# A recommender tower on one core: 24 interaction rows kept, dense features in the free rows of the pair chunks

## What is computed

```python
combined = jnp.concatenate([sparse_x, dense_x[:, None, :]], axis=1)      # 512 x 27 x 128
interact = jnp.einsum('bfd,bgd->bfg', combined, combined)
z = interact[:, _TRIU_I, _TRIU_J]                                        # 512 x 351
h = jnp.concatenate([z, r_dense_x], axis=1)                              # 512 x 479
h = jnp.maximum(h @ W_top1 + b_top1, 0.0)                                # 479 x 512
h = jnp.maximum(h @ W_top2 + b_top2, 0.0)                                # 512 x 256
y = h @ W_top3                                                           # 256 x 1
```

## Time and profile before

| | before |
|---|---|
| median of 3 runs | 120.97 us (120.47 to 121.06) |
| the profiled execution | 120.48 us |
| its span, first to last instruction | 118.7 us |
| TensorE busy | 110.9 us, 93% (weight loads 88.0, 74%) |
| VectorE busy | 93.1 us, 78% |
| ScalarE busy | 50.6 us, 43% |
| GpSimd busy | 71.6 us, 60%, none of it after 96.72 |
| granted TensorE clock | 1.0 throughout |
| moved | 13.20 MB, 111 GB/s on average |

### The profile page before, as it was taken

How to read it: one execution, slowest core, us unless ns; L and a number is a source line. 1 busy time by engine, 2 the same in 40 slices (tenths; PEclk the granted TensorE clock), 3 DMA queues, 4 the chain that set the end, 5 groups by cost and what they waited for, 6 DMA issues and landing times.

```text
span 118.7 us, 2740 instructions
## 1 busy us (share of the span) xinstructions
PE 110.9 (93%) x794; PEld 88.0 (74%) x794; DVE 93.1 (78%) x379; ACT 50.6 (43%) x147; POOL 71.6 (60%) x80
## 2 busy tenths in 40 slices
PE   4999999999999999999989999799999996999990
PEld 4844454546454799759979898699998895998980
DVE  1699999999999998984999999940689992589312
ACT  5970640506050618930355871105686104586110
POOL 3477777777777776776777777776777750000000
PEclk9999999999999999999999999999999999999999
DMA  3999757454535125897321221221221220000000
GB/s 83 303 319 383 205 168 242 76 215 88 184 111 181 51 68 96 321 355 226 72 51 46 67 45 50 52 63 45 61 59 46 61 50 0 6 0 0 0 0 1
DMA packets 6543, 13.20 MB, mean 111 GB/s; under 512 B 2033, under 2 KB 3569, under 8 KB 6401
## 3 DMA queue, kind: packets, MB, share of 16 engines
q0 software_dynamic: 2336, 4.79, 15.1%
q1 hardware_dynamic: 3328, 5.50, 13.9%
q10 hardware_dynamic: 864, 2.75, 7.5%
HBM read 13.03 MB, written 0.00 MB: 110 GB/s over the span
## 4 chain that ended last, share of the span: by engine, by line
POOL 58%; issue 19%; PE 14%; DMA 5%; POOLq 1%; DVE 1%; ACT 0%; DVEq 0%
POOL rows L329 58%; PE gram_ps L625 6%; PE h_ps L660 3%; DMA idx<-in_ids_dram 3%; DMA rows<-in_tbl_dram,idx 2%; PE turn_ps L645 2%; PE h_ps L645 1%; POOLq L102 1%; PE gram_ps L645 1%; PE turn_ps L631 0%; DVE h L485 0%; DVE h_prod L487 0%; PE turn_ps L598 0%; ACT XT L374 0%; PE gram_ps L631 0%
## 5 line engine op out<-in xcount | busy, mean ns | idle before, releaser
L329 POOL DMA_INDIRECT rows<-in_tbl_dram,idx x73 | 70.5, 966 | 24.0 <-issue 22.0
L430 DVE COPY PAIRS<-gram_ps 27x60 f32<-27x60 f32 (+1 forms) x96 | 24.3, 253 | 11.6 <-PE gram_ps L625 10.2
L625 PE MATMUL gram_ps<-XT 128*123 128x80 f32 x256 | 28.5, 269 | 1.2 <-ACT XT L374 0.9
L625 PEld LDWEIGHTS gram_ps<-XT 128*123 128x123 f32 x256 | 27.9, 188 | 2.0 <-ACT XT L374 1.4
L374 ACT COPY PAIRS<-gram_ps 27x60 f32<-27x60 f32 (+1 forms) x96 | 23.3, 243 | 10.3 <-PE gram_ps L625 9.2
L374 ACT COPY XT<-turn_ps 128x512 f32<-128x512 f32 (+3 forms) x20 | 12.2, 619 | 34.3 <-PE turn_ps L598 18.2
L455 DVE CUSTOM_DVE_ANT_0 few_prod<-rows 128x128 f32<-128x128 f32 x84 | 20.6, 289 | 0.8
L513 DVE TENSOR_SCALAR onehot<-hot_ids,first_row 125x512 bf16<-125x512 int16 (+1 forms) x64 | 19.4, 374 | 2.4 <-DMA hot_ids<-in_hot_ids_dram 2.1
L645 PE MATMUL h_ps<-PAIRS,W1P 128*128 128x128 f32 x130 | 16.8, 276 | 0.2
L645 PEld LDWEIGHTS h_ps<-PAIRS,W1P 128*128 128x128 f32 x130 | 15.5, 192 | 0.5 <-ACT PAIRS L374 0.3
L588 PE MATMUL turn_ps<-onehot,hot_tab 125*128 125x512 bf16 (+3 forms) x56 | 11.7, 351 | 0.0
(11 more groups left out here) (49 smaller groups left out, 87.0 us busy)
## 6 DMA issues: line engine op xcount, KB each, us to landing
hot_tab<-in_hot_dram ACTq DMA_DIRECT2D x5, 512.0 KB, 3.6
rows<-in_tbl_dram SPq DMA_DIRECT2D x128, 0.5 KB
W1P<-in_w_pairs_dram SPq DMA_DIRECT2D x1, 1280.0 KB, 5.9
rows<-in_tbl_dram,idx POOLq DMA_INDIRECT x73, 2.9
hot_tab<-in_hot_dram SPq DMA_DIRECT2D x2, 512.0 KB, 7.4
hot_ids<-in_hot_ids_dram SPq DMA_DIRECT2D x1, 640.0 KB, 7.5
hot_tab<-in_hot_dram SPq DMA_DIRECT2D x2, 256.0 KB, 3.4
W<-in_W_top_dram SPq DMA_DIRECT2D x1, 512.0 KB
```

The source lines that it names most:

```text
L329: pool.indirect_dma_start(rows[:, t, s, :], None, tables[f], bass.IndirectOffsetOnAxis(ap=idx[:, t, f:f + 1], axis=0)) \
L430: return nc.vector.tensor_copy(dst, src)
L625: last = nc.tensor.matmul(gram_ps[0:GRAM_ROWS, 2 * (i % 2) + q // fours, o:o + QUAD * NCOL], four.rearrange("d s f -> d (s f)")[:, 0:GRAM_ ...
```

## The change

It makes these edits:

- **24 rows.** The slots of each sample are filled in another order: dense, the fields of gather groups 1 to 6, the hot fields, and last the three fields of group 0. `move_pairs` copies 24 partitions, `gram` has 3 x 32 + 24 = 120 stationary columns. Pairs among the last three slots are in no copied row, so `FEW` grows from 21 to 24 and each part from seven pairs to eight. The pairs now come from gather groups 0, 1 and 2, not 0 and 1.
- **Free rows.** A quadrant now has eight free rows. The 24 few pairs all fit in those of chunk 0: one turn and one addition are left of two. Chunks 1 to 4 have 4 x 8 x 4 = 128 free rows, which take the dense input. Four loads on SP's queue, eight partitions and 2048 floats each, write it from `x_t`. W1's dense rows are in `W1P`; `W1D` and its product are gone. ScalarE clears chunk 0 alone.
- **First loads.** ScalarE's load of the first ids moves to SP's queue behind the index; ids come as [0], [1], [2:8] instead of [0], [1:3], [3:8]; table 2 comes ahead of the dense input. The copy of the dense input into `XT` moves behind ScalarE's fifth bank.
- **Warm-up.** Nine matmuls on a tile of zeros cleared by VectorE, in place of eight on the identity.
- **Turns of tile 0** move up: [1, 2], [3, 4], [5, 6], [].

```diff
-FEW = [(a, g) for g in range(FIRST) for a in range(g)]
+KEPT = 24
+APART = NVEC - KEPT
+FEW = [(a, g) for g in range(KEPT, NVEC) for a in range(KEPT, g)] + [(a, g) for g in range(FIRST) for a in range(g)]
...
-GRAM_ROWS = SLOTS * (QUAD - 1) + NVEC
+GRAM_ROWS = SLOTS * (QUAD - 1) + KEPT
...
-WARM_UP = 8
+WARM_UP = 9
 RING = 3
+DENSE_AFTER = 4
...
-SLOT_FIELD = [NTAB] + COLD + HOT
+ROW_FIELD = [NTAB] + COLD
+SLOT_FIELD = [NTAB] + COLD[APART:] + HOT + COLD[:APART]
+ROW_SLOT = [SLOT_FIELD.index(f) for f in ROW_FIELD]
...
-TURNS_AFTER = [[[1], [2, 3], [4, 5], [6]], [[1, 2], [3, 4], [5], []], [[1, 2], [5], [3], [4]]]
+TURNS_AFTER = [[[1, 2], [3, 4], [5, 6], []], [[1, 2], [3, 4], [5], []], [[1, 2], [5], [3], [4]]]
...
             sp.dma_start(idx[:], ids).then_inc(idx_in, 16)
+            sp.dma_start(hot_ids[:, 0, :], hot_ids_in[:, 0, :]).then_inc(ids_first_in, 16)
...
-            sp.dma_start(hot_ids[:, 1:3, :], hot_ids_in[:, 1:3, :]).then_inc(ids_next_in, 16)
+            sp.dma_start(hot_ids[:, 1, :], hot_ids_in[:, 1, :]).then_inc(ids_next_in, 16)
             load_hot(sp, 1)
+            sp.dma_start(hot_ids[:, 2:n_look, :], hot_ids_in[:, 2:n_look, :]).then_inc(ids_rest_in, 16)
+            load_hot(sp, 2)
...
             sp.dma_start(W1P[:], w1_pairs).then_inc(w1_in, 16)
-            sp.dma_start(W1D[:], w1_dense).then_inc(w1_in, 16)
+            for s in range(4):
+                sp.dma_start(PAIRS[SLOTS * s + KEPT:SLOTS * (s + 1), 1:PART_COLS, :],
+                             x_t.rearrange("(s i k) b -> s i k b", s=4, i=SPARE)[s]).then_inc(dense_pairs_in, 16)
...
-            act.dma_start(hot_ids[:, 0, :], hot_ids_in[:, 0, :]).then_inc(ids_first_in, 16)
             act.wait_ge(few_cleared, 1)
-            zero_pairs(0, PART_COLS // 2)
-            zero_pairs(PART_COLS // 2, PART_COLS)
...
+            nc.scalar.activation(PAIRS[:, 0, :].rearrange("p (t s) -> p t s", t=TILES),
+                                 few[:, 0:1, 0:P].broadcast_to([P, TILES, P]), ACT.Identity).then_inc(pairs_zero, 1)
...
-                nc.vector.tensor_tensor(PAIRS[0:SLOTS, 1, here], PAIRS[0:SLOTS, 1, here],
-                                        few_bank[t][0:SLOTS, P:2 * P], ALU.add).then_inc(turn_read["dve"], 1)
...
+            pe.wait_ge(warm_ready, 1)
+            for _ in range(WARM_UP):
+                nc.tensor.matmul(h2_ps[:, 0:P], warm[:], warm[:], start=True, stop=True)
             pe.wait_ge(ident_ready, 1)
...
-            def layer1_dense(t, n):
-                nc.tensor.matmul(h1_out(t, n), W1D[:, n * P:(n + 1) * P], denseT[:, t * P:(t + 1) * P],
-                                 start=True, stop=False)
...
-                order = list(range(FEW_CHUNKS, PART_COLS)) + list(range(FEW_CHUNKS))
+                order = [*range(1, PART_COLS), 0]
...
-                    pe.wait_ge(w1_in, 32)
+                    pe.wait_ge(w1_in, 16)
+                    pe.wait_ge(dense_pairs_in, 16 * 4)
```

More of the change, by code:

```diff
@@ L120, in build @@
         W1P = sb("W1P", [P, PART_COLS, H1], F32)
-        W1D = sb("W1D", [P, H1], F32)
         W2 = sb("W2", [P, HC1, H2], F32)
@@ L340, in empty_bank @@
                 _, n, a, b = item
-                slot = TURNED + n if n < n_hot else TURNED - 1
+                slot = SLOT_FIELD.index(LOOKUPS[n])
                 copy(XT[:, a * P:b * P, slot], ps[:, 0:(b - a) * P]).then_inc(turn_read[reader[i]], 1)
@@ L437, in few_pairs @@
                     if t == 0:
-                        dve.wait_ge(pairs_zero, 2)
+                        dve.wait_ge(pairs_zero, 1)
                     dve.wait_ge(dense_in, 16)
+                go = FEW[part * FEW_GO:(part + 1) * FEW_GO]
                 for g in range(NG):
-                    if GROUPS[g][0] < FIRST:
+                    if any(ROW_SLOT[r] in pair for r in GROUPS[g] for pair in go):
                         dve.wait_ge(gathered[g], 16 * gather_count(g) * (t + 1))
@@ L453, in few_pairs @@
                         dve.wait_ge(few_step, step - 1)
-                    col = few_place(i)[1] * P + few_place(i)[0]
+                    col = few_place(i)
                     nc.vector.tensor_tensor_reduce(
-                        out=few_prod[:, step % 2, :], in0=rows[:, t, a, :], in1=rows[:, t, g, :], scale=1.0,
+                        out=few_prod[:, step % 2, :], in0=rows[:, t, ROW_SLOT.index(a), :], in1=rows[:, t, ROW_SLOT.index(g), :], scale=1.0,
                         scalar=0.0, op0=ALU.mult, op1=ALU.add,
@@ L466, in add_few @@
                 dve.wait_ge(turned, fill_no[("few", t)] + 1)
[L467 to L469 removed]
+                nc.vector.tensor_tensor(PAIRS[:, 0, here], PAIRS[:, 0, here], few_bank[t][:, 0:P],
+                                        ALU.add).then_inc(turn_read["dve"], 1)
             def relu_dve(t, n):
@@ L551, in _ @@
         def _(pe):
+            pe.wait_ge(warm_ready, 1)
+            for _ in range(WARM_UP):
+                nc.tensor.matmul(h2_ps[:, 0:P], warm[:], warm[:], start=True, stop=True)
             pe.wait_ge(ident_ready, 1)
-            for _ in range(WARM_UP):
-                nc.tensor.matmul(h2_ps[:, 0:P], ident[:], ident[:], start=True, stop=True)
             def bank_free(i):
@@ L645, in layer1_pairs @@
                     last = nc.tensor.matmul(h1_out(t, n), W1P[:, k, n * P:(n + 1) * P], PAIRS[:, k, t * P:(t + 1) * P],
-                                            start=False, stop=(k == order[-1]))
+                                            start=(k == order[0]), stop=(k == order[-1]))
                 if t == TILES - 1 or n == HC1 - 1:
@@ L696, in _, with weight_rows @@
                         fill(late_hot)
-            pe.wait_ge(pairs_act, BATCHES * (t + 1) - 1)
-            pe.wait_ge(pairs_dve, BATCHES * (t + 1) - 1)
-            for n in range(HC1 - 1):
-                layer1_dense(t, n)
             for n in range(HC1):
-                if n == HC1 - 1:
-                    layer1_dense(t, n)
-                layer1_pairs(t, n)
+                layer1(t, n)
             layer2(t)
 def few_place(i):
-    chunk, i = divmod(i, FEW_PER_CHUNK)
     quadrant, row = divmod(i, SPARE)
-    return SLOTS * quadrant + NVEC + row, chunk
-def pair_rows():
+    return SLOTS * quadrant + KEPT + row
+def weight_rows():
     rows = []
@@ L724, in pair_rows @@
             a, g = sorted((slot[i], slot[j]))
-            if g < FIRST:
-                rows.append((*few_place(FEW.index((a, g))), n))
+            if (a, g) in FEW:
+                rows.append((few_place(FEW.index((a, g))), 0, n))
             else:
@@ L730, in pair_rows @@
             n += 1
-    return rows, n
+    for d in range(D):
+        s, i, k = d // (SPARE * (PART_COLS - 1)), d // (PART_COLS - 1) % SPARE, d % (PART_COLS - 1)
+        rows.append((SLOTS * s + KEPT + i, 1 + k, n + d))
+    return rows
 def kernel(**inputs):
@@ L760 @@
     w1 = _np.asarray(inputs["W_top1"])
-    where, n_pairs = pair_rows()
-    p, k, r = (_np.array(c) for c in zip(*where))
+    p, k, r = (_np.array(c) for c in zip(*weight_rows()))
     w1_pairs = _np.zeros((P, PART_COLS, H1), w1.dtype)
@@ L765 @@
     w1p = give("w1_pairs", w1_pairs)
-    w1d = give("w1_dense", w1[n_pairs:])
     b1 = give("b_top1", _np.asarray(inputs["b_top1"]).reshape(HC1, P).T)
@@ L771 @@
     out = nc.dram_tensor("out_0_dram", (BATCH, 1), _mybir.dt.float32, kind="ExternalOutput").ap()
-    build(nc, x, x_t, ids, row_ids, hot_ids, hot_tables, tables, w1p, w1d, b1, w2, b2, w3, out)
+    build(nc, x, x_t, ids, row_ids, hot_ids, hot_tables, tables, w1p, b1, w2, b2, w3, out)
     r = _run(nc, [arrays], core_ids=[0])
```

54 lines of the change are left out of this document (23 added, 31 removed).

## The result

The changed kernel took 126.73 us (median of 4 runs, 126.17 to 126.78), the kernel before 121.02 us (120.47 to 121.75) beside it. The ratio is 1.050, its 95% interval 1.046 to 1.054: slower by 5.7 us, where 120.9 was forecast.

What follows compares the result with a forecast made beforehand. Gathers bound the last interactions (99.42), with VectorE and TensorE close. L of 53.6 plus 46.10 starts them 0.28 late, the tail gains 0.32: -0.04, so 120.9 us against the median; range 120.4 to 121.7.

Steps and rivals of the forecast that it cites:

- Dense rows by four loads into the pair chunks: Tile 0, before layer one: W1P lands at 52.43, the dense loads at 53.5, so layer one starts at 53.6.
- L: Start of layer one in tile 0, its first pair matmul: forecast 53.6, from 53.2 to 53.8.
- the term of 1.1: Time in us by which the four dense loads land behind W1P, taken between 0.75 and 1.5.
- The bound of 1.5: Upper bound in us for the dense loads landing behind W1P, at half of W1D's rate: landing 53.95.
- Rival 2: VectorE waits in tile 0 for turn 1 behind the dense loads and passes it on: 122.0 us, chance 0.15.
- The sum along VectorE: Spans added from layer one's start in tile 0 to the last interactions: together 46.10 us.
- ready for layer one: TensorE in tile 0, after VectorE's longer first tile: ready at 53.27, where before it was 52.50.
- The tail: From the last interactions to the end: gain 0.32 us, 19.0 instead of 19.28.
- Tile 1's wait for VectorE: Sign: TensorE waits more than 1 us for VectorE's copies in tile 1, 0.21 before.
- Rival 3: GpSimd's gathers start sooner, the index landing 0.4 sooner: 120.5 us, with shorter copies up to -0.8; chance 0.13.
- the turning point: L of 53.32, above which VectorE instead of the gathers sets the start of the last interactions.
- the last gather should land within 0.3 of 98.41: Sign: GpSimd's last indirect gather, ahead of the last tile's interactions, lands about where it did before, at 98.41.

Runs made afterwards that it cites:

- the kernel with the filled wait: The changed kernel with 18 matmuls on the zero tile ahead of TensorE's wait in tile 0: 125.71 us, ratio 1.044.
- the run at full clock: The changed kernel with W1P, the four loads and the other weights issued behind row fetch 31 instead of 63: 126.34 us, ratio 1.043.

## Why the prediction was wrong

**The step that failed** is "Dense rows by four loads into the pair chunks". It took W1P's landing from its old 5.9 us (52.43) and put the dense loads 0.75 to 1.5 us behind it, 1.1 as my value, hence L = 53.6. Measured, the loads were in at 57.96. From W1P's issue at 46.76 that is 11.20 us, where the prediction had 5.9 + 1.1: the term of 1.1 was 5.3, nearly five times too small. The split between the two is not steady (W1P was complete at 54.86 in this trace, after 8.1 us, but after 6.3 in the probe and 6.5 in the kernel with the filled wait), while the sum is: 11.20, 11.72 and 10.93. The bound of 1.5 was not a bound. It was the price of W1D's bytes at half rate, and came from a row with 128 partitions for a load that has eight. The probe with those loads alone reproduces the delay (+5.02 us in the kernel before, +4.50 here).

The rule of the Trainium skill that the prediction weighed, half the DMA engines for eight partitions (DMA: Bandwidth & Descriptors), pointed the right way and was far too mild. The traces agree with its count: each load of eight partitions ended with eight increments from DMA engines, each of 16, 32 or 128 with sixteen. But half the rate for 256 KB is 0.75 us more, and the same rule gives 16 partitions all engines. Measured against one load of 128 partitions, eight cost 3.56 more and sixteen 1.39 more: the packets themselves took longer, and the number of engines doesn't cover that.

**What was not in the sum at all** is the clock. The forecast had TensorE's pace at its row before for the whole program. After 4.08 us of waiting, ten instructions took 1.97 us and eight turns 1.71 (1.12 and 0.87 at full clock), so that the copy of turn 1 came 3.07 behind L and not 1.75, which is what it is at full clock (53.73 to 55.48 with the weights early). That is 1.32, the L-to-last-interactions stretch is longer by 1.20 than in the run at full clock (47.59 against 46.39), and the four executions at full clock with the wait filled were 0.7 to 1.0 shorter.

**What was right.**
- Rival 2 had the mechanism: VectorE waits in tile 0 for turn 1 behind the dense loads and passes each tenth on to the end. Its price was too low: 122.0, with the loads 2.25 us behind W1P where 5.3 was measured. Its chance of 0.15 was too small for it.
- The sum along VectorE was 46.10. At full clock it measured 46.39, 46.43 and 46.55 in three kernels (the last with its dense product kept): 0.3 to 0.5 too short in 46.
- TensorE was to be ready for layer one at 53.27; it was ready at about 53.7. VectorE's copies began at 45.65, not 45.0, since the first ids arrived 0.69 later (4.61 against 3.92) and not 0.4. That is partly chance: with the same first loads other traces have the ids at 3.85 to 3.96 and the copies at 44.5 to 44.6.
- The tail was to gain 0.32 and gained 0.43. Tile 1's wait for VectorE (0.94, forecast "more than 1") and turn 5's in tile 2 (0.74) are there.
- Rival 3's mechanism happened: the gathers start 0.9 to 1.4 us sooner, against the 0.4 assumed. It could not show in the time, since the turning point had moved from the gathers to VectorE. Alone, moving the first ids is worth 1.4 us, and it is the only part of the change that was seen to pay: the changed kernel with its loads early and the clock kept up took 120.62, not less than before. The sentence "the last gather should land within 0.3 of 98.41" was wrong by this.

With the right L of 57.96, the prediction's own sum gives 104.06 for the last interactions and, with the tail, +4.3 us: the loads explain three quarters of the loss. The clock (0.7 to 1.2) and the 0.3 that the sum missed are about the rest.

## What to carry to other kernels

Moving rows of 128 partitions into free rows of another tile can cost more than the product that it saves: here 0.88 us of TensorE a tile against 4.5 us of transfer on the path (of the whole program, once). Ask of each load how many partitions it writes and what is in flight beside it, and measure such a load alone, as a probe in the old kernel, before the change is built on it. Price a new wait on TensorE twice, once as time and once as the clock that may be lower behind it (here 0.7 to 1.2 us behind 4.08, and 4.9 behind 1.64); and try each small part of a change by itself, since the one that pays (a load less beside the index) may be hidden under the one that costs.
